# Another order of TensorE's work around the start and the projections of the state-space units, and the products of probabilities and values one tile later

## The reference, cut to what matters

```
h = exp(dt_t * A) * h + (dt_t * u_t) * B_t
y_t = einsum('bdn,bn->bd', h, C_t)
y = (y + u * D) * silu(z);  out = y @ Wout.T
```

```
probs = softmax(where(causal, q.k * scale, min))
attn = probs @ v;  x = x + attn @ wo.T
out = sum over e of (silu(h@w1)*(h@w3)) @ w2 * wfull[:, e]
```

## Time and profile before

| | |
|---|---|
| median of 3 runs | 1731.54 us (1727.22 to 1733.29) |
| profiled execution | 1731.18 us, span of its instructions 1729.4 us |
| PE busy | 1354.6 us, 78% of the span |
| DVE busy | 1376.4 us, 80% |
| ACT busy | 1047.1 us, 61% |
| POOL busy | 1112.5 us, 64% |
| mean granted clock of PE | 0.879 |

### The profile page before, as it was taken

The page is one execution under the profiler, slowest core; times in us unless marked ns, Lnnn a source line. Parts: engine busy times, 40 slices in busy tenths (PEclk is TensorE's granted clock), DMA queues, the critical chain, the costliest instruction groups (busy, mean ns, idle before and its releaser), DMA issues. The chain is left out here.

```text
span 1729.4 us, 30919 instructions
## 1 busy us (share of the span) xinstructions
PE 1354.6 (78%) x8880; PEld 983.0 (57%) x8880; DVE 1376.4 (80%) x2250; ACT 1047.1 (61%) x1856; POOL 1112.5 (64%) x1244
## 2 busy tenths in 40 slices
PE   5878787778778777886887668888988888888771
PEld 2656566556656565665666433344665555656671
DVE  2999899999999999999999745667678777777432
ACT  6777676776776776777768214556555655546330
POOL 1777777787777777777878713435457466554535
PEclk8889899898889888898988656879899999999886
DMA  5112302320222123023203021133556455454762
GB/s 189 56 52 99 123 10 89 122 98 18 104 98 75 48 98 123 0 98 123 88 16 139 25 83 30 49 101 126 174 166 200 146 180 165 139 191 142 230 220 71
DMA packets 115274, 186.05 MB, mean 108 GB/s; under 512 B 10736, under 2 KB 87536, under 8 KB 110960
## 3 DMA queue, kind: packets, MB, share of 16 engines
q1 hardware_dynamic: 111056, 176.30, 29.7%
q0 software_dynamic: 4096, 8.40, 1.7%
HBM read 153.92 MB, written 26.15 MB: 104 GB/s over the span
## 5 line engine op out<-in xcount | busy, mean ns | idle before, releaser
L883 DVE TENSOR_TENSOR_SCAN wt<-da,dbu 128x512 f32<-128x512 f32 x448 | 528.2, 1206 | 30.6 <-PE dbu L454 21.7
L721 ACT ACTIVATE da<-dt,a_neg 128x512 f32<-128x512 f32 x512 | 353.0, 716 | 194.1 <-DVE wt L883 162.8
L1027 POOL TENSOR_TENSOR hc<-wt,qk 128x512 f32<-128x512 f32 x256 | 328.3, 1300 | 99.8 <-DVE wt L883 80.2
L1027 POOL TENSOR_TENSOR hc<-wt,cb 128x512 f32<-128x512 f32 x256 | 326.5, 1295 | 95.0 <-DVE wt L883 83.5
L493 PE MATMUL yp<-ident,hc 128*128 128x128 f32 x2048 | 328.6, 296 | 5.3 <-POOL hc L1027 5.1
L493 PEld LDWEIGHTS yp<-ident,hc 128*128 128x128 f32 x2048 | 279.1, 156 | 81.1 <-issue 48.6
L2020 ACT ACTIVATE pt<-scores,lift 128x512 f32<-128x512 f32 x320 | 216.8, 684 | 172.4 <-PE scores L1763 170.7
L2151 DVE TENSOR_REDUCE mx<-wp 128x1 f32<-128x384 f32 (+3 forms) x352 | 218.2, 636 | 102.5 <-PE wp L1725 97.7
L867 DVE TENSOR_TENSOR dbu<-dtu,bp 128x512 f32<-128x512 f32 x384 | 251.5, 685 | 18.4 <-PE bp L481 9.5
L2498 POOL TENSOR_SCALAR_AFFINE_SELECT pt<-pt 128x256 f32<-128x256 f32 (+1 forms) x320 | 119.5, 376 | 196.1 <-ACT pt L2020 195.0
L403 PE MATMUL wp<-xpad,wu 128*128 128x512 f32 x256 | 133.1, 612 | 11.5 <-DVE wt L898 6.5
(11 more groups left out here) (251 smaller groups left out, 2477.6 us busy)
## 6 DMA issues: line engine op xcount, KB each, us to landing
wt<-ffn_w_e SPq DMA_DIRECT2D x120, 384.0 KB, 4.5
qk<-c_scratch SPq DMA_DIRECT2D x8, 3072.0 KB, 12.1
cb<-c_scratch SPq DMA_DIRECT2D x8, 3072.0 KB, 11.7
qk<-q_scratch SPq DMA_DIRECT2D x96, 96.0 KB
qk<-c_scratch SPq DMA_DIRECT2D x8, 1024.0 KB, 4.5
cb<-c_scratch SPq DMA_DIRECT2D x8, 1024.0 KB, 4.8
xg<-xs_scratch SPq DMA_DIRECT2D x24, 256.0 KB, 3.3
ys_scratch<-ysb SPq DMA_DIRECT2D x24, 256.0 KB, 2.5
```

The costliest lines, as they stand in the source:

```text
L721: nc.scalar.activation(da[:, s % NDA, :], dt[:, h, :], ACT.Exp, scale=a_neg[:, d, h, n:n + 1]).then_inc(da_done, 1)
L883: nc.vector.tensor_tensor_scan(hb[:, s % NHB, :], da[:, s % NDA, :], src, 0.0, ALU.mult, ALU.add).then_inc(scan_done, 1)
L1027: nc.gpsimd.tensor_tensor(hc[:, s % NHC, :], hb[:, s % NHB, :], cb[d][:, s // 2, :], ALU.mult).then_inc(hc_done, 1)
```

## The change

On PE, `pe_dtt` moves behind the tail's `pe_y` 27 and 28, and `pe_b(1)` moves from step 1 to step 0, between these two. So ahead of the wait for dtu there are now y 27, B of state 1 and y 28. In the front, z moves from steps 19 and 20 to 20 and 21, xd from 21 to 23, dt from 24 and 25 to 25 and 26, the transpose of B from 24 to 25. On ACT the block of silus moves from step 25 to 24. In the second phase the three groups of products stand one slot later: 6, 10 and 12.

```diff
@@ pe_unit
                 if s % 2 == 1 and s // 2 + 1 < NS:
                     if made_by_pe(d, s // 2 + 1):
                         pe_fill(pe, b, d, s // 2 + 1, 0)
-                    else:
+                    elif s > 1:
                         pe_b(pe, b, d, s // 2 + 1)
...
+                if tail and s == 0:
+                    pe_y(pe, *tail, STEPS - LAG_Y)
+                if s == 0:
+                    pe_b(pe, b, d, 1)
+                if tail and s < LAG_Y - 1:
+                    pe_y(pe, *tail, STEPS - LAG_Y + 1 + s)
                 if s == 0:
                     pe_dtt(pe, b, d)
-                if tail and s == 0:
-                    pe_y(pe, *tail, STEPS - LAG_Y)
-                if tail and s < LAG_Y - 1:
-                    pe_y(pe, *tail, STEPS - LAG_Y + 1 + s)
...
-                    if s in (19, 20):
-                        pe_z(pe, *front, s - 19)
-                    if s == 21:
+                    if s in (20, 21):
+                        pe_z(pe, *front, s - 20)
+                    if s == 23:
                         pe_xd(pe, *front)
-                    if s in (24, 25):
-                        pe_dt(pe, *front, s - 24)
-                    if s == 24:
+                    if s in (25, 26):
+                        pe_dt(pe, *front, s - 25)
+                    if s == 25:
                         pe_bt(pe, *front)
@@ act_front
-            if at == 25:
+            if at == 24:
                 act_silu_u(act, b, d, 0)
@@
-PV_AT = ((5, (0, 1, 2, 3)), (9, (4, 5, 6, 7)), (11, (8, 9)))
+PV_AT = ((6, (0, 1, 2, 3)), (10, (4, 5, 6, 7)), (12, (8, 9)))
```

## The result

The changed kernel takes 1738.65 us (median of 20 runs, 1734.47 to 1753.67), the kernel before beside it 1732.91 us (20 runs, 1714.27 to 1742.57): 1.0053 of before, 95% interval 1.0032 to 1.0073. I had said 1718.5 us and "faster". The profiled execution takes 1738.44 us, its span is 1736.7 us.

A forecast was written before the change was run, and what follows sets the result against it. DVE's work plus waits bound the first phase; loops between engines, with no engine full, the second. From 1731.2 us, -18.75 (front), +1.4 (unit's start) and +4.7 (products) gave 1718.5 us, range 1703 to 1732.

The forecast's parts named there:

- place (a): Slot 19, second phase: products now follow the gate's wait, which grows to 2.9 us; +5.4 us over 5 places.
- Products one slot later: Second phase, three product groups moved to even slots behind an expert step: sum +4.7 us, bounds -22.4 and +30 us.
- fourth rival: Products behind even slots' waits lose 3.6 us in each of 7 sequences, front's gain lost: 1754 us; chance 0.10.
- place (b): Slot 42, second phase: last products now follow the expert step, DVE's sums wait 0.6 us; +2.3 us after halving.
- -3.0 for POOL's waits in the first and last sequences: Second phase: a quarter of 11.4 us of PE's waits for POOL's mask there was counted as won.
- The front: State-space phase, z, xd, dt and silus reordered: DVE's waits for the fill and B nearly go, gain 18.75 us.
- The unit's start: y 27, 28 and B of state 1 ahead of dtu's wait: direct gain 0, clock loss in one more unit, +1.4 us.
- third rival: Work in the gap at a unit's start keeps 2.4 GHz: -5.5 in place of +1.4, 1711.6 us; chance 0.12.
- first rival: Products' wait for the mask was on the way, half of 22.4 us won: 1702.7 us; chance 0.15.
- The second: Rival: xd late behind fill(12, 0) and y 18, fill(12, 1) as late as before: 1733.6 or 1726 us; chance 0.13.
- The checks of the last part: Signs in the changed trace: silu wait 3.2 to about 1 us, mask wait nearly gone, h2tn wait 2.9, period up about 1.

The follow-up runs named there:

- e10: Changed kernel with the product of scores ahead of the gate written 14 times, filling the gap: 1726.2 us, 0.9987 of the kernel before.
- e1: Changed kernel with the products back in their old slots, so the state-space part alone: 0.9935 of the kernel before, 0.9881 when run beside the changed kernel.
- e2: Kernel before with only the products one slot later, old order of the state-space phase: 1749.1 us, 1.0178 of the kernel before.
- e4: Changed kernel with only the middle group of products late (slots 5, 10, 11): 1723.0 us, 1.0055 of the kernel before.
- e7: State-space part with only the first group of products late (slots 6, 9, 11): 1702.3 us, 0.9898 of the kernel before.
- e8: State-space part with only the last group of products late (slots 5, 9, 12): 1706.6 us, 0.9929 of the kernel before.
- e6: Changed kernel with products in the same late slots, but issued ahead of the gate and the expert step: 1695.8 us, 0.9862 of the kernel before.
- e11: e6 with the gap at the gate filled by 8 repeats of a matmul: 1704.4 us, 0.9860 of the kernel before.
- e12: e1 with repeated products of scores filling the waits of slots 19 and 20: 1695.4 us, 0.9846 of the kernel before.
- e14: Kernel before, nothing moved, with repeated matmuls ahead of z and in slots 19 and 20: 1708.6 us, 0.9857 of the kernel before.
- e13: Kernel before, nothing moved, with the broadcast of B for state 10 ahead of z written 9 times: 1713.4 us, 0.9893 of the kernel before.

## Why the prediction was wrong, point by point

- **What failed** is place (a) of "Products one slot later". I wrote "it grows to 1.19 + 1.07 + 0.61 = 2.9 us, and 1.07 us of work comes after it. 5 places x 1.07 = +5.4 us". The wait grew to 2.96 us in just that place, at four of the eight gates. What I left out is that behind these 2.96 us of idle PE the granted clock was 0.50 to 0.72, so the work there runs at or near 1.2 GHz: 15.6 us more of busy time over five periods than in the first profile of before (4.9 more than in the second), of which e10 gave 13.7 back, and about 11 us of time. The whole term was +4.7 us and measured 24 to 30 (e1 against the changed kernel, e2 alone). The clock is shown as a cause of that, not as the whole of it.
- I had the mechanism in my hand, in the earlier trace rows, and used it for the first phase only. The earlier trace rows give 0.87 for the second phase, and the kernel before already lost its clock in two of five periods.
- The idle time beside it was +9.4 us over five periods, and it is not the +5.4 us of place (a). By what ended PE's waits in these stretches, those ahead of the gate rose from 1.8 to 12.2 us, but those for the mask fell from 11.8 to none: together 1.4 us less. What rose is elsewhere in the even slots: the waits for g (L1853) from none to 8.9, for nmr (L1702) from none to 4.2, for ga (L1875) from 6.4 to 9.8; the waits for x, ot and the keys' DMA fell. My sum had nothing for these, only the fourth rival did. The waits for g and nmr come with the first group: e4, without it, has none, e7, with it alone, has 8.9 and 4.2 us. But e7's ratio is near e1's, so what they cost in time is not shown. The price of place (b), +2.3, was not measured by itself; e8, the last group alone late, is within the scatter of e1. The -3.0 for POOL's waits in the first and last sequences can't be told apart either.
- **The front** was priced at -18.75 us. The phase became 23.0 us shorter against the profile that I had, 13 us against the second. My figure lies between the two, so that it is near either is partly luck. The reason was half of it: I explained 1.65 us by the order of z, xd and dt ahead of the fill, where most of it was PE at half clock behind the wait for the silu. Filling the gap without a move gives the same.
- **The unit's start**: +1.4 predicted, -0.3 us measured alone (1003.6 against 1003.9). The third rival's gain, B of state 5 and fill(4, 1) in time, came true: no wait for B has a row left in the first profile. Its cause is not the work put into the gap, since the front moves alone have it (one wait for B, 0.5 us) and the start alone does not (7.1 us in 7). At the start of the unit around 566 us the clock still falls, to 0.50.
- **The first rival** (the mask's wait was on the way) is not borne out by the change and not settled by e6: that kernel halves the wait for the mask, but its 0.9862 (0.9833 to 0.9892) overlaps the second measurement of e1, which has the whole wait. **The second** did not come: xd stood behind two more steps and was in time. **The fourth** had the right kind of place and the right sign, at 0.10 and without the clock: "3.6 us in each of 7 sequences" was measured as 3.5 to 8 us in four of the five periods.
- The checks of the last part: the silu's wait 3.2 to 1 us (measured 1.36), the mask's wait nearly gone (4.7 of 22.4 us), the gate's 2.9 (2.96) were all right. A period growing by 1 us was wrong: it grew by 3.5 to 8 us.

The Trainium skill ("TensorE: Matmul & The Clock Gate", Part 1, What's actually happening) says that PE's recent activity sets its clock. Here the traces agree in the main: behind 2.96 us of idleness the granted clock was 0.50 to 0.72, and with work put into that wait it was 1.00 behind every gate (e10, e11, e12).

What stays open is why the clock falls at one gate and holds at another behind the same 11 us of rows (e8). The falls that e10 and e11 kept are at other waits of the period, which nobody filled, and the one that e14 kept at a gate (0.72) is at the fourth, where 0.88 us of wait was left; why e12 had none at all is not explained. Open too is how the 24 us between e1 and the changed kernel divide between the clock and the waits themselves, beyond the 11 us that e10 gave back.

## What to carry to other kernels

When a step is moved behind a wait, price the wait twice: once as idle time, and once as PE's clock behind it, by comparing the same row (here sixteen products at 1.07 and at 1.94 us) behind long and short waits in the trace at hand. Ask of each longer wait of PE what the rows behind it cost, before explaining a late result by the order of the queue. If a wait can't be removed, a move that splits it, or even repeated matmuls in it, can be worth more than the work saved.

## What the runs showed that I had not expected

- Repeating a matmul made a kernel faster: by 6.9 us in the old order (e12 against e1, one chip), by 18 to 21 us in the kernel before (e13, 0.9893; 21 by the medians), and the changed kernel from 1.0053 to 0.9987 (e10). It did nothing that can be measured for e6 (e11), and e14's 0.9857 overlaps e13's.
- The spread of the kernel before on one chip, 1698 to 1733 us in 29 runs, has the clock in it: its executions show granted clocks from 0.903 in one of 1698.3 us to 0.876 in one of 1731.9 us. In its second profile the first two pairs of units ran 3 us shorter than the later ones. The changed kernel, which loses the clock at each gate, spreads less: 1722.7 to 1732.6 us in 12 runs, where the kernel before beside it had 1709.8 to 1731.0 in 17.
